# Samples work of the next batch ahead of the output projection, and six pieces of the next first layer made inside the end of the batch

## What is computed

```python
for (cw, cb, gw, gb), (_, _, s) in zip(conv_params, CONV_LAYERS):   # 6 layers, 128 channels
    h = gelu(group_norm_32(conv1d(h, cw, stride=s) + cb) * gw + gb) # strides 5,2,2,2,2,2
h = h.transpose(0, 2, 1) @ pw.T + pb                                # (4, 749, 192)
h = h + attention(layernorm(h))                                     # 12 heads of 64, causal
h = h + mixture(layernorm(h))                                       # expert = argmax(x @ gate_w + gate_b) of 8
```

## Time and profile before

| | |
|---|---|
| three runs, median | 1612.37 us |
| lowest, highest | 1612.15, 1617.33 us |
| the profiled execution, its own time | 1609.28 us |
| its span in the profile | 1607.5 us |
| TensorE busy | 1416.6 us (88%) |
| VectorE busy | 1068.1 us (66%) |
| ScalarE busy | 778.8 us (48%) |
| GpSimd busy | 408.2 us (25%) |

### The profile page before, as it was taken

The page is one execution under the profiler, slowest core; times in us unless marked ns, Lnnn a source line. Parts: engine busy times, 40 slices in busy tenths (PEclk is TensorE's granted clock), DMA queues, the critical chain, the costliest instruction groups (busy, mean ns, idle before and its releaser), DMA issues.

```text
span 1607.5 us, 29299 instructions
## 1 busy us (share of the span) xinstructions
PE 1416.6 (88%) x10191; PEld 978.7 (61%) x10192; DVE 1068.1 (66%) x2482; ACT 778.8 (48%) x1490; POOL 408.2 (25%) x425
## 2 busy tenths in 40 slices
PE   5987799998987799998987799999886899969997
PEld 3333378886433488884443588883433788856665
DVE  4988655557987555568896555659886555664553
ACT  1664355643654456525563565616643666532332
POOL 3000044513000244403000334302000576721222
PEclk8899899998998899997989999989998999979999
DMA  5997033210000122201000223200000643222221
GB/s 135 344 352 247 1 73 74 53 36 31 12 1 0 39 69 50 69 12 42 1 1 1 58 56 73 50 1 30 1 1 1 156 120 87 52 68 55 64 61 32
DMA packets 109553, 104.81 MB, mean 65 GB/s; under 512 B 51772, under 2 KB 99961, under 8 KB 109425
## 3 DMA queue, kind: packets, MB, share of 16 engines
q1 hardware_dynamic: 80210, 54.53, 14.1%
q10 hardware_dynamic: 25744, 39.62, 7.5%
q0 software_dynamic: 3472, 8.97, 1.6%
HBM read 28.78 MB, written 47.40 MB: 47 GB/s over the span
## 4 chain that ended last, share of the span: by engine, by line
PE 49%; DVE 28%; issue 10%; POOL 5%; ACT 4%; DMA 2%; SPq 2%; POOLq 0%; DVEq 0%; ACTq 0%
PE ps L1879 12%; DVE arena L1301 10%; PE ps L1929 8%; PE ps L1859 7%; DVE arena L1299 6%; PE ps L1869 6%; DVE bn L1458 4%; PE ps L1812 4%; PE ps L1973 3%; PE ps L1818 2%; DMA arena<-arena 2%; SPq L573 1%; POOL out L900 1%; ACT arena L1002 1%; POOL arena L797 1%
## 5 line engine op out<-in xcount | busy, mean ns | idle before, releaser
L1929 PE MATMUL ps<-arena,cwt 128*128 128x504 f16 (+2 forms) x1776 | 391.6, 381 | 40.8 <-DVE arena L1299 38.7
L1929 PEld LDWEIGHTS ps<-arena,cwt 128*128 128x128 f16 x1776 | 175.5, 102 | 257.1 <-DVE arena L1299 42.3
L1320 DVE TENSOR_REDUCE nmax<-ps 128x1 f32<-128x128 f32 (+5 forms) x288 | 173.5, 615 | 116.6 <-PE ps L1862 116.6
L1879 PE MATMUL ps<-arena 128*128 128x64 f32 (+2 forms) x2016 | 237.8, 270 | 2.6 <-DVE arena L1328 2.6
L1879 PEld LDWEIGHTS ps<-arena 128*128 128x128 f32 (+2 forms) x2016 | 229.9, 188 | 8.3 <-DVE arena L1328 4.2
L1301 DVE TENSOR_TENSOR arena<-arena 128x1008 f16<-128x1008 f32 (+4 forms) x200 | 227.1, 1136 | 6.9
L980 ACT ACTIVATE arena<-ps,nmax 128x128 f32<-128x128 f32 (+5 forms) x288 | 181.2, 630 | 58.9 <-DVE nmax L1320 56.3
L1328 DVE COPY arena<-ps 128x512 f32<-128x512 f32 (+4 forms) x288 | 152.1, 535 | 70.0 <-PE ps L1869 67.0
L1042 ACT ACTIVATE arena<-ps 128x1008 f32<-128x1008 f32 (+1 forms) x112 | 96.1, 866 | 179.8 <-PE ps L1929 179.8
L1859 PE MATMUL ps<-arena 128*128 128x512 f16 (+6 forms) x780 | 154.5, 310 | 19.2 <-DMA arena<-arena 10.4
L786 POOL TENSOR_TENSOR tmp<-tmp,neg_half 128x1 f32<-128x1 f32 x24 | 13.3, 553 | 545.4 <-DVE tmp L1202 545.4
(11 more groups left out here) (291 smaller groups left out, 2242.6 us busy)
## 6 DMA issues: line engine op xcount, KB each, us to landing
slot_scratch<-empty_slot ACTq DMA_DIRECT2D x1, 38692.5 KB, 119.9
arena<-arena SPq DMA_DIRECT2D x96, 187.5 KB, 3.0
arena<-arena SPq DMA_DIRECT2D x96, 93.8 KB, 2.4
arena<-in_L_ffn_w SPq DMA_DIRECT2D x16, 288.0 KB, 6.7
arena<-in_L_ffn_w SPq DMA_DIRECT2D x8, 576.0 KB, 7.5
arena<-slot_scratch SPq DMA_DIRECT2D x31, 96.5 KB, 1.9
arena<-slot_scratch SPq DMA_DIRECT2D x31, 96.0 KB, 1.9
xa<-in_x POOLq DMA_DIRECT2D x4, 468.8 KB, 4.7
```

Of the source, the lines that this page charges most:

```text
L1320: v.reduce_max(nmax[0:m, k:k + 1], banks_at(("S", p, k))[0:m, 0:128 * i + m], AX.X, negate=True).then_inc(S["smax_done"], 1)
L1879: last = t.matmul(bank_at(BANKS[job][0])[0:m, 0:DH], probt[(STEPS * p + k) % PROBTS][0:kk, c, 0:m], vt[0:kk, c, DH * hh:DH * hh + DH], sta ...
L1929: last = t.matmul(bank(g, k)[:, 0:c * PITCH].rearrange("p (r c) -> p r c", c=PITCH), cwt[layer][:, w, tap, :], parts[x][:, f:f + 2 * c - 1 ...
```

## The change

Three things change, with the semaphore counts that follow from them.

1. The samples work of the next batch stands ahead of the output projection in `post_jobs`, and `split_samples` ahead of the last `TC` on VectorE. The projection's two parts change places: tiles 4 and 5 first. The bias `bo_b` is added to `h` behind `chan`. GpSimd makes the group's power ahead of the layer norm's.
2. Pieces 0 to 5 of the next layer 0 are made in the end of the batch: three after `group`, two after the first part of the projection, one between the two gate jobs. VectorE's splits of them stand behind the group norm, the variance, the copy of the token transposes, and the choice of the expert. The next tower begins with layer 1. For batch 0 the set-up makes these pieces.
3. TensorE's waits at the start of the end of the batch are for the last readers of the banks in question (`LAST_HOLDER`), where they were for all of attention's.

```diff
+AHEAD = 6
+def first_conv0(some):
+    return [("conv0", (piece // 3, piece % 3), (ACT_ENGINE,)) for piece in some]
 def tower_jobs():
...
-        jobs += [("conv0", (j, i), (ACT_ENGINE,)) for i in range(3)]
+        jobs += first_conv0(range(max(AHEAD, 3 * j), 3 * j + 3))
...
 def post_jobs():
-    jobs = [("wo", (0,), (DVE_ENGINE,)), ("wo", (1,), (DVE_ENGINE,))]
-
     xt0, xt1, gram, taps, chan, group = samples_jobs()
-    jobs += [xt0, xt1, gram, ("tr", (0,), (DVE_ENGINE,)), ("tr", (1,), (ACT_ENGINE,)), taps,
-             chan, ("gate", (0,), (DVE_ENGINE,)), group, ("gate", (1,), (DVE_ENGINE,)), ("rank", (), (DVE_ENGINE,))]
-    return jobs
+    wo0, wo1, tr0, tr1, gate0, gate1, rank = last_post_jobs()
+    ahead = first_conv0(range(AHEAD))
+    jobs = [gram, xt0, taps, xt1, chan, wo1, group] + ahead[:3] + [wo0] + ahead[3:5]
+    return jobs + [tr0, tr1, gate0, ahead[5], gate1, rank]
...
             def end_of_batch(b, phase=POST):
-                wait(pool, "var_ready", phase, 1, b)
+                if phase == POST:
+                    group_rstd(POST, 1, b)
+                wait(pool, "var_ready", phase, COUNTS["var_ready"][PHASES.index(phase)], b)
                 g.tensor_tensor(lnr[:, :], lnv[:, :], neg_half[:, 0:TT], ALU.pow).then_inc(S["rstd_ready"], 1)
...
+                if b < BATCH - 1:
+                    a.activation(spare[:, 30:31], ones_col[:, :], ACT.Gelu_apprx_tanh)
                 for g, n, kind, args in jobs_of(post):
+                    if kind == "conv0":
+                        gelu_of_first_layer(post, g, n, args, b, b + 1)
+                        continue
...
+            def split_ahead(phase, piece, b, tower):
+                made = job_index(phase, "conv0", (piece // 3, piece % 3))
+                wait(dve, "act_freed", phase, freed(phase, ACT_ENGINE, made), b)
+                split((0, piece), tower)
...
-                if b < BATCH - 1:
-                    split_samples(POST, b)
-                for i in range(TT):
-                    m = tile_rows(i)
-                    last = v.tensor_tensor(h[0:m, i, :], h[0:m, i, :], bo_b[0:m, :], ALU.add)
-                step(last)
+                for kind, p, k in ATT_DVE:
+                    if (kind, p) == ("TC", PAIRS - 1) and b < BATCH - 1:
+                        split_samples(POST, b)
+                    attention_step(kind, p, k, b)
...
                         samples_job(POST, n, b)
+                        if kind == "chan":
+                            add_output_bias()
+                        elif kind == "group":
+                            for piece in range(3):
+                                split_ahead(POST, piece, b, b + 1)
                         continue
...
-                            final_layernorm((lambda: w1a_low(2)) if b == BATCH - 1 else
-                                            lambda: samples_job(POST, job_index(POST, "xt", (0,)), b))
+                            final_layernorm(tiles, (lambda: w1a_low(2)) if b == BATCH - 1 else
+                                            lambda: split_ahead(POST, 3, b, b + 1))
...
-                elif phase in (POST, LAST_POST) and n == 0:
+                elif phase == POST and n < 4:
+                    first = 2 * (slot_of(POST, n) % 4)
+                    takers = [taken_by(*LAST_HOLDER[x], x) for x in (first, first + 1)]
+                    wait_for_takers(takers, b)
+                elif phase == LAST_POST and n == 0:
                     wait(pe, "act_freed", phase, 0, b)
                     wait(pe, "dve_freed", phase, 0, b)
```

More of the change, by code:

```diff
@@ L231, with split_no @@
 STAGES = 4
+def split_no(unit):
+    return SPLITS.index(unit) + 1 - AHEAD
 COUNTS = {
@@ L1044, in _ @@
                     elif kind == "conv0":
[L1045 to L1058, removed]
+                        gelu_of_first_layer(TOWER, g, n, args, b, b)
                     elif kind in ("q", "k", "v"):
@@ L1239, in token_norms, with final_layernorm @@
                 return last
-            def final_layernorm(meanwhile):
-                step(token_stats(range(4, TT)))
+            def final_layernorm(tiles, meanwhile):
+                step(token_stats(tiles))
                 carry_wait()
@@ L1666, in _, with wait_for_takers @@
             t = nc.tensor
+            def wait_for_takers(takers, b):
+                by_act = [ACT_NTH[x] for x in takers if x[0] not in ("CP", "TC")]
+                by_dve = [DVE_NTH[x] for x in takers if x[0] in ("CP", "TC")]
+                if by_act:
+                    wait(pe, "act_freed", ATT, max(by_act), b)
+                if by_dve:
+                    wait(pe, "dve_freed", ATT, max(by_dve), b)
             def slot_free(phase, n, b=None):
@@ L1745, in samples_job, with first_layer @@
                 last.then_inc(S["ps_full"], 1)
+            def first_layer(phase, n, args, b=None):
+                j, i = args
+                g = slot_of(phase, n)
+                if phase != TOWER:
+                    wait(pe, "dve_freed", phase, freed(phase, DVE_ENGINE, job_index(phase, "xt", (0,))), b)
+                for k in range(2):
+                    last = t.matmul(bank(g, k)[:, 0:4 * PITCH], cw0t[:, 2 * i + k, :],
+                                    xt[:, 4 * j:4 * j + 4, :].rearrange("p k c -> p (k c)"),
+                                    start=True, stop=True)
+                return last
             pe.wait_ge(consts_ready, N_CONSTS)
@@ L1899, in _ @@
                     if kind == "conv0":
-                        j, i = args
-                        for k in range(2):
-                            last = t.matmul(bank(g, k)[:, 0:4 * PITCH], cw0t[:, 2 * i + k, :],
-                                            xt[:, 4 * j:4 * j + 4, :].rearrange("p k c -> p (k c)"),
-                                            start=True, stop=True)
+                        last = first_layer(TOWER, n, args, b)
                     elif kind == "group":
@@ L1967, in _ @@
                         continue
-                    if kind == "wo":
+                    if kind == "conv0":
+                        last = first_layer(POST, n, args, b)
+                    elif kind == "wo":
+                        wait(pe, "dve_freed", post, 0, b)
                         tiles = range(4) if args[0] == 0 else range(4, TT)
```

83 lines of the change are left out of this document (54 added, 29 removed).

## The result

The change makes the kernel slower: 1646.74 us median of 4 runs (1645.84 to 1650.52), beside 1614.82 us for the kernel before on the same chip (1612.15 to 1617.33, 4 runs; the forecast was added to 1612.37, the median of the first three). The ratio is 1.0204, with a 95% interval of 1.018 to 1.0228. The forecast was 1635 us with a range to 1645; the time lies 1.7 us above that range. Counted from 1614.82 in place of 1612.37, the range would end 0.7 us above it. The direction was right, and of the cases named it is rival 2: the change costs 31.9 us where 22.7 was forecast.

The account below looks back on a forecast made before the run. VectorE was taken to bound the tower part, TensorE after the change. Each of three batches cost +4.3 us (99.5 against 95.0, less 0.2 rounding), plus 9.8 for clock falls: 1612.4 + 22.7 = 1635 us, range 1614 to 1645.

Parts of the forecast that it names:

- rival 2: Clock falls around Gram matrix and projection in all three batches, or comes back later: 1640 to 1654 us; chance 0.15.
- The tower part: Layers 0 and 1 of the next tower: falls from 61.8 to 55.9 us at full clock, with TensorE the bound.
- the low start: Start of the tower: the half clock level, formerly hidden, now puts 2.5 us on the path.
- The end of the batch: From `TC` through projection, layer norm, gate and rank: 41.1 us, before any price for an early clock fall.
- the early fall: Clock falls to half around the Gram matrix, ahead of the projection: +4.9 us in a batch where it comes.
- split 3: VectorE's split behind the layer norm's variance: 1.89 us, covered by GpSimd's power but for 0.5.
- I count it in two of three batches: The clock fall ahead of the projection, counted in two batches: 2 x 4.9 = 9.8 us.
- the signs that I had named: 99 to 105 us from `TC` to layer 1's statistics, VectorE idle in tower, TensorE idle 6 us, level 0.50.
- Covered at nothing: VectorE's samples split, some 2.5 us, ahead of `TC`: costed at nothing, since VectorE waited there for `ZT`.
- Rivals 1: Clock level holds through Gram matrix and projection: +13 us, 1625 us; chance 0.17.
- 4: Low level in one batch alone, no measurable change: 1613 to 1617 us; chance 0.10.
- Rival 3: TensorE keeps full clock from projection into tower: -1.7 us a batch, 1607 us; chance 0.08.

Follow-up runs that it names:

- e7: The change with four pieces ahead, second half of sample transposes behind the projection, 25 products without a use added; 1610.55 us, 0.9973 of the kernel before.
- e2: The change plus 24 matmuls without a use in TensorE's wait for the layer norm, ahead of the token transposes; 1632.99 us, 1.0118 of the kernel before.
- e5: The change's order with no pieces ahead, plus a wait of the Gram matrix for the last `TC`; 1658.15 us, 1.0261 of the kernel before.
- e1: The change plus five matmuls without a use in TensorE's wait ahead of the Gram matrix; 1629.27 us, 1.0091 of the kernel before.
- e4: The change's order alone, with no first-layer pieces ahead, so the Gram matrix gets a free slot; 1635.86 us, 1.0129 of the kernel before.
- e9: The change with all six pieces plus two empty jobs, which move every job's PSUM slot by two; 1627.79 us, 1.0083 of the kernel before.
- e3: The change plus matmuls without a use both ahead of the Gram matrix and ahead of the token transposes; 1622.21 us, 1.0035 of the kernel before.
- e8: The kernel before plus 4 products without a use ahead of the first gate part and 7 ahead of rank; 1617.08 us, 1.0024 of the kernel before.

## Where the prediction held, and the step that failed

**The tower part**: right, to a tenth. 55.9 at full clock and 2.5 for the low start were forecast, 58.4 measured; TensorE waits for VectorE 0.4 us in it. It is the bound now, which e7 bears out from the other side: the same stretch at 1.00 takes 57.3 us, with four pieces ahead in place of six.

**The end of the batch**: the order of steps was right, the sum too small. With the early fall I had 41.1 + 4.9 = 46.0 us; it is 47.8. By step from the start of the Gram matrix (356.80): all samples work 11.8 us, where 7.9 and 3.6 were forecast; the end of the projection's first part at 27.4 for 26.3, since the second part took 6.02 us for 5.3 and the samples work 0.3 us more than forecast (the wait for its slot came as forecast, 1.5 us for 1.6); the token transposes at 34.4 for 33.3, behind the forecast 6 us of idle time (6.21); the gate at 38.1 for 36.0, since I gave the two transposes "a little more at half clock", and they took 2.8 us for 1.5, with a copy behind them. Gate, choice and rank were forecast at 10.0 and took 9.7. That is 1.8 us a batch, 5.4 in all: terms that were mis-sized, the half clock in the projection's second part and in the token transposes above all. The working of the layer norm also names 0.5 us of split 3 that its sum, 21.4 + 7.0 = 28.4, leaves out; the stretch took 7.1 us for those 7.0.

**The step that failed** is "I count it in two of three batches, since a batch can begin the Gram matrix early enough at the high level". All three batches fell, 0.5 to 2.0 us into the Gram matrix, each for about 13.7 us, and so did all of e2 and e5. The third is worth 4.9 us by my own price, and with it and the 1.8 us a batch the forecast would have been 1645 us, or 33.0 us of loss for 31.9 measured. The price itself was low: e1, without the fall, is 5.5 us shorter up to rank in the first batch, where I had taken 4.9. Of the signs that I had named, the idle time, the level in gate and tower and VectorE's new idle time are there; the 99 to 105 us became 106.2. Of the 37.6 us between the two profiled executions, what lies outside the edited stages is in stages that hold no edit (from the group norm of layer 1 to the next last `TC` 761.9 us for three batches in place of 759.2, 2.6 in the first tower and attention, and 0.9 behind the last `TC`).

Behind that step is a deeper one, though its facts stood in the text: "Its slot shares a PSUM bank with `ZT`, so the wait of 1.19 us in front of it stays". I named the wait and the thin work behind it together as the reason for a fall, but took the wait as given and as free, because it had been there before. e4, e5 and e9 show that it is what decides in this order. The same wait ahead of 12 us of dense projection brought no fall in two of before's three batches; the same thin work without the wait keeps the level for 18.6 us; both together cost 1.1 to 1.3% of the kernel (e1, e9, e5). The number that mattered was how many jobs stand in the list, since that chooses the slot, and six pieces make it 19. I had not asked what the slot would be with another number.

**Covered at nothing**: VectorE's split of the samples ahead of `TC` cost nothing, as forecast (VectorE is still idle for 0.65 us ahead of `TC` at 355.67, waiting for `ZT`). The set-up cost 0.1 us: the first norm of layer 1 is at 102.05 us for 101.94.

**The rivals.** Rivals 1 and 3 supposed a level that holds, and 4 a low level in one batch alone; the windows refute each for this order. The outcome is rival 2, to which I gave 0.15. Rival 3 is what e3 and e7 build by hand: it priced the full clock at -1.7 us a batch against before, and e7, with the level held from Gram matrix to gate, has 94.43 us from `TC` to the norm for 96.15. That this is its price is in part luck: e7 also has a free slot, four pieces, half of the transposes in the wait and 25 products without a use.

The Trainium skill, "TensorE: Matmul & The Clock Gate", section "Why this matters for your kernels", on gaps that throw the engine back: e5 against e4 agrees in direction, a gap of 1.09 us being the whole edit. But that gap is shorter than those of which the section warns, and in front of the projection of before such a gap mostly did nothing, so the measurement and not the rule decides here. Its section "Part 4: PE-mode transpose", by which transposes are no work to the gate, would have given the early fall in all three batches, as it came. It would not have told e4 from e5, whose transposes are the same; in e4 they lie within 18.6 us at 1.00.

What stays open: why the level falls at 376.6 in e8 although TensorE is busy for 9.6 of the 10 us ahead of it, while e4 holds through 18.6 us with a similar mix. And e3 is still 0.35% slower than before; its gate runs at half from 388 on, and I did not separate that from the order. Nor was a version run that has the pieces ahead and the order of before, so what the pieces alone would bring there is not shown.

## What to carry to other kernels

Read the clock ahead of a stretch of small matmuls as a term of its own: a stall of 1 us brought the low level in one of six places in front of dense work here, and in nine of nine in front of thin work, where it cost 7 us. When jobs take buffers by their number, adding or removing a job moves every other job's buffer; list which job comes to share one with whom before you count waits as unchanged. And work that hides a wait has a second value if it keeps TensorE going: taking 7.9 us of it away from under a layer norm left 6 us idle and the clock at half for 20 us, where before had 14 to 17.

## What the hardware showed that I had not expected

- One wait of 1.09 us ahead of the Gram matrix (e5) halves TensorE's clock for over 13 us in each batch, and 5 products without a use in such a wait (e1, 1.24 us) prevent that in all three: 1.1% of the kernel.
- Products added where the level is at half cost their doubled price: in e8 seven took 3.02 us, at full clock (e7) 14 took 3.18.
- In e8 the level falls directly behind 10 us in which TensorE was busy for 9.6.
